# Cross attention: two tiles' output projections in one score slot, a chunk's gate logits in one slot

## What is computed

```python
x = layernorm(x + linear_self_attention(x))          # 2048 rows of 256
x = layernorm(x + cross_attention(x, ctx, ctx))      # 16 heads of 16, 1601 keys
x = layernorm(x + moe(x))                            # 16 experts, the 4 best for a row, and a shared one

def cross_attention(query, key, value):
    Q, K, V = heads(query @ Wq + bq), heads(key @ Wk + bk), heads(value @ Wv + bv)
    attn = softmax(Q @ K.T / 4)
    return merge(attn @ V) @ Wo + bo                 # "@ Wo" is the output projection of the change

probs = softmax(x @ gate_w.T)                        # "x @ gate_w.T" are the gate logits of the change
```

## Time and profile before

| | |
|---|---|
| timed runs, median (lowest to highest of 3) | 1037.9 us (1035.8 to 1038.04) |
| the profiled execution | 1044.55 us, its span 1042.7 us |
| busy: PE, DVE, ACT, POOL | 943.0, 749.9, 646.4, 264.1 us |
| main loop | about 240 to 795 us of the span |
| chunk 1 starts (step 0), chunk 2, chunk 3 | 372.3, 511.7, 653.3 us |
| L1206 PE, a pass of the projection | x48, 0.38 to 0.48 us each |
| L874 ACT, copy of a projection | x12, 0.38 us each |
| L746 POOL, addition of a projection | x8, 0.68 us each (median) |
| L1227 PE, a pass of the logits | x48, 0.26 us each (median) |
| L885 ACT, copy of two tiles' logits | x6, 0.20 us each |

### The profile page before, as it was taken

How to read it: one execution, slowest core, us unless ns; L and a number is a source line. 1 busy time by engine, 2 the same in 40 slices (tenths; PEclk the granted TensorE clock), 3 DMA queues, 4 the chain that set the end, 5 groups by cost and what they waited for, 6 DMA issues and landing times.

```text
span 1042.7 us, 19228 instructions
## 1 busy us (share of the span) xinstructions
PE 943.0 (90%) x6870; PEld 514.8 (49%) x6870; DVE 749.9 (72%) x1230; ACT 646.4 (62%) x1405; POOL 264.1 (25%) x354
## 2 busy tenths in 40 slices
PE   6997899769999999999999999999999999898790
PEld 2453566424444444444444444434434887676660
DVE  0205888598999998989998989988971544333694
ACT  1322233206888888888887888867788565556460
POOL 1006011900000001020012420023243446654564
PEclk9999999957999999999999999999989999999895
DMA  9007895110333434010001110112345354435863
GB/s 347 20 1 136 132 114 138 41 61 1 94 104 100 108 98 125 8 28 22 25 19 49 48 43 18 27 32 75 103 138 153 93 148 138 132 119 150 271 212 136
DMA packets 75508, 99.29 MB, mean 95 GB/s; under 512 B 17276, under 2 KB 58492, under 8 KB 75098
## 3 DMA queue, kind: packets, MB, share of 16 engines
q1 hardware_dynamic: 63960, 73.73, 27.8%
q0 software_dynamic: 7584, 20.79, 5.4%
q10 hardware_dynamic: 3872, 3.56, 1.0%
HBM read 52.45 MB, written 43.35 MB: 92 GB/s over the span
## 4 chain that ended last, share of the span: by engine, by line
PE 65%; DVE 20%; issue 5%; DMA 3%; ACTq 2%; ACT 2%; SPq 1%; POOL 1%; another core or an unknown queue 0%; POOLq 0%; DVEq 0%
PE psum L1182 17%; PE psum L1072 13%; DVE mpart L1485 10%; PE psum L1168 8%; PE psum L1337 7%; PE psum L1355 4%; PE psum L1034 3%; PE psum L1298 2%; PE psum L1001 1%; ACTq L802 1%; PE psum L1122 1%; PE psum L1206 1%; DMA kparts_d<-region 1%; PE psum L1008 1%; PE psum L1196 1%
## 5 line engine op out<-in xcount | busy, mean ns | idle before, releaser
L956 ACT ACTIVATE region<-psum 128x512 f32<-128x512 f32 (+1 forms) x832 | 448.4, 604 | 127.6 <-PE psum L1168 113.0
L1485 DVE TENSOR_REDUCE mpart<-psum 128x2 f32<-128x1024 f32 x384 | 460.1, 1222 | 35.8 <-PE psum L1072 31.8
L1182 PE MATMUL psum<-region 128*32 128x256 f32 (+1 forms) x3120 | 250.5, 393 | 1.8
L1072 PE MATMUL psum<-kstack,qstack 63*128 63x512 f32 (+1 forms) x1024 | 222.4, 462 | 20.7 <-DVE mpart L1485 18.0
L1072 PEld LDWEIGHTS psum<-kstack,qstack 63*128 63x128 f32 x1024 | 92.2, 192 | 194.8 <-issue 125.7
L1168 PE MATMUL psum<-qstack,kstack 64*128 64x512 f32 (+1 forms) x832 | 176.2, 414 | 0.1
L1168 PEld LDWEIGHTS psum<-qstack,kstack 64*128 64x128 f32 (+1 forms) x832 | 111.2, 185 | 17.5 <-ACT region L956 10.7
L1745 DVE SCALAR_TENSOR_TENSOR silu_h<-tanh_h,psum 128x128 f32<-128x128 f32 x110 | 31.6, 287 | 119.8 <-ACT tanh_h L926 89.9
L1182 PEld LDWEIGHTS psum<-region 128*32 128x32 f32 (+1 forms) x3120 | 62.1, 108 | 112.0 <-issue 80.0
L708 POOL DMA_INDIRECT given_d<-y_out,x_in x94 | 93.1, 990 | 84.1 <-ACT y_out L940 59.3
L1337 PE MATMUL psum<-w_all,xT_in 128*128 x376 | 100.0, 389 | 9.5 <-issue 7.1
(11 more groups left out here) (197 smaller groups left out, 955.6 us busy)
## 6 DMA issues: line engine op xcount, KB each, us to landing
x_in<-sorted_d SPq DMA_DIRECT2D x94, 129.0 KB
sorted_d<-x_in SPq DMA_DIRECT2D x7, 1548.0 KB, 7.8
given<-given_d SPq DMA_DIRECT2D x16, 512.0 KB
qstack<-qparts_d SPq DMA_DIRECT2D x96, 64.0 KB, 2.3
kstack<-kparts_d SPq DMA_DIRECT2D x6, 800.5 KB
qparts_d<-region SPq DMA_DIRECT2D x4, 1024.0 KB, 4.1
kparts_d<-region SPq DMA_DIRECT2D x4, 800.5 KB, 10.1
xT<-in_xT SPq DMA_DIRECT2D x1, 2048.0 KB, 8.9
```

What stands on the lines that cost most here:

```text
L956: act.activation(prob[0:rows_of, s % 3, j, :], ring(n)[0:rows_of], ACT.Exp).then_inc(ring_read, 1)
L1072: mm = pe.matmul(bank(unit_bank(u) + side)[:, at * w:(at + 1) * w], qstack[rows_of, buffer(G), p, t * P:(t + 1) * P], kstack[rows_of, g * ...
L1182: mm = pe.matmul(bank(NUM_BANK)[VW * j:VW * (j + 1), q], vals[0:r, g, kt, j, :], prob[0:r, s % 3, j, q], start=(kt == 0 and half == 0), st ...
L1485: dve.tensor_reduce(mpart[:, G % 2, qt, :, p, n], both, X, ALU.max).then_inc(max_read, 1)
```

## The change

Two tiles' projections share a slot. Their results lie side by side in one bank (2 x 256 columns), and ScalarE copies both in one instruction. `PROJ_AT` becomes (12, 18); in chunk 3 the two slots stand at steps 12 and 14. The four tiles' logits share a slot at step 34 (chunks 1 and 2) or 23 (chunk 3), and steps 36 and 24 lose theirs. GpSimd's additions move from steps 13, 16, 19, 22 to 13, 14, 19, 20; VectorE's statistics from 15, 18, 21, 24 to 15, 16, 21, 22. In chunk 3 VectorE's steps stay. The products, the additions and the statistics are the same in number.

```diff
-        PROJ_AT = (12, 15, 18, 21)
+        PROJ_AT = (12, 18)
+        PROJ_TILES = TPC // len(PROJ_AT)
...
-                jobs = ([(12 + t, "proj", t) for t in range(TPC)]
-                        + [(4, "rank", 1), (20, "x2T", 0), (21, "x2T", 1), (23, "logits", 0), (24, "logits", 1),
-                           (32, "rank", 2)])
+                jobs = [(12, "proj", 0), (14, "proj", 1), (4, "rank", 1), (20, "x2T", 0), (21, "x2T", 1),
+                        (23, "logits", 0), (32, "rank", 2)]
             else:
-                jobs = ([(PROJ_AT[t], "proj", t) for t in range(TPC)]
-                        + [(30, "x2T", 0), (32, "x2T", 1), (34, "logits", 0), (36, "logits", 1)]
+                jobs = ([(at, "proj", n) for n, at in enumerate(PROJ_AT)]
+                        + [(30, "x2T", 0), (32, "x2T", 1), (34, "logits", 0)]
...
-                        if at == PROJ_AT[t] + 1:
+                        if at == PROJ_AT[t // PROJ_TILES] + 1 + t % PROJ_TILES:
                             add_attention(c - 1, t)
...
-            def copy_proj(c, t, n):
+            def copy_proj(c, part, n):
+                first, end = PROJ_TILES * part, PROJ_TILES * (part + 1)
                 act.wait_ge(ring_full, n + 1)
                 if c >= 1:
-                    act.wait_ge(co_read, TPC * (c - 1) + t + 1)
-                act.activation(proj[:, t, :], ring(n)[:, 0:DIM], ACT.Copy).then_inc(ring_read, 1)
+                    act.wait_ge(co_read, TPC * (c - 1) + end)
+                act.activation(proj[:, first:end, :].rearrange("p t n -> p (t n)"), ring(n)[:, 0:PROJ_TILES * DIM],
+                               ACT.Copy).then_inc(ring_read, 1)
...
-                for k in range(DK):
-                    mm = pe.matmul(ring(n)[:, 0:DIM], attnT[:, k, t * P:(t + 1) * P], wo_c[:, k, :],
-                                   start=(k == 0), stop=(k == DK - 1))
+                for q in range(PROJ_TILES):
+                    t = PROJ_TILES * part + q
+                    for k in range(DK):
+                        mm = pe.matmul(ring(n)[:, q * DIM:(q + 1) * DIM], attnT[:, k, t * P:(t + 1) * P], wo_c[:, k, :],
+                                       start=(k == 0), stop=(k == DK - 1))
                 mm.then_inc(ring_full, 1)
...
-                for q in range(2):
-                    t = 2 * half + q
+                for t in range(TPC):
                     for k in range(DK):
-                        mm = pe.matmul(ring(n)[:, q * EXPERTS:(q + 1) * EXPERTS], x2T[:, k, t * P:(t + 1) * P],
+                        mm = pe.matmul(ring(n)[:, t * EXPERTS:(t + 1) * EXPERTS], x2T[:, k, t * P:(t + 1) * P],
                                        gate_wT[:, k, :], start=(k == 0), stop=(k == DK - 1))
                 mm.then_inc(ring_full, 1)
...
-                        if at == PROJ_AT[t] + 3:
+                        if at == PROJ_AT[t // PROJ_TILES] + 3 + t % PROJ_TILES:
                             attended_stats(c - 1, t)
```

More of the change, by code:

```diff
@@ L739, in divide @@
                 if c >= 1 and k == 0:
-                    pool.wait_ge(ring_full, extra_slot("proj", (c - 1, TPC - 1)) + 1)
+                    pool.wait_ge(ring_full, extra_slot("proj", (c - 1, len(PROJ_AT) - 1)) + 1)
                 pool.tensor_tensor(attnT[:, k, :], num_c[:, k, :], den_c[:, k, :], ALU.mult).then_inc(attn_ready, 1)
@@ L744, in add_attention @@
                 at = TPC * c + t
-                pool.wait_ge(ring_read, extra_slot("proj", (c, t)) + 1)
+                pool.wait_ge(ring_read, extra_slot("proj", (c, t // PROJ_TILES)) + 1)
                 pool.tensor_tensor(x_sb[:, at, :], proj[:, t, :], x_sb[:, at, :], ALU.add).then_inc(co_read, 1)
@@ L878, in copy_x2T, with copy_logits @@
                 if c >= 1:
-                    act.wait_ge(ring_full, extra_slot("logits", (c - 1, 1)) + 1)
+                    act.wait_ge(ring_full, extra_slot("logits", (c - 1, 0)) + 1)
                 act.activation(x2T[:, k, :], ring(n), ACT.Copy).then_inc(ring_read, 1)
-            def copy_logits(c, half, n):
+            def copy_logits(c, n):
                 act.wait_ge(ring_full, n + 1)
-                at = TPC * c + 2 * half
-                act.activation(logits[:, at:at + 2, :].rearrange("p t e -> p (t e)"),
-                               ring(n)[:, 0:2 * EXPERTS], ACT.Copy).then_inc(ring_read, 1)
+                act.activation(logits[:, TPC * c:TPC * (c + 1), :].rearrange("p t e -> p (t e)"),
+                               ring(n)[:, 0:TPC * EXPERTS], ACT.Copy).then_inc(ring_read, 1)
             def copy_rank(stage, n):
@@ L963, in _ @@
                 elif what == "logits":
-                    copy_logits(*arg, n)
+                    copy_logits(arg[0], n)
                 elif what == "rank":
@@ L1198, in weigh_whole, with out_proj @@
                 mm.then_inc(pv_done, 1)
-            def out_proj(c, t, n):
+            def out_proj(c, part, n):
                 pe.wait_ge(attn_ready, DK * (c + 1))
                 ring_free(n)
-                if c == 0 and t == 0:
+                if c == 0 and part == 0:
                     pe.wait_ge(ld_woc, 16)
-                for k in range(DK):
-                    mm = pe.matmul(ring(n)[:, 0:DIM], attnT[:, k, t * P:(t + 1) * P], wo_c[:, k, :],
-                                   start=(k == 0), stop=(k == DK - 1))
+                for q in range(PROJ_TILES):
[3 more added lines that the diff above has]
+                                       start=(k == 0), stop=(k == DK - 1))
                 mm.then_inc(ring_full, 1)
@@ L1216, in turn_x2, with gate_logits @@
                 mm.then_inc(ring_full, 1)
-            def gate_logits(c, half, n):
+            def gate_logits(c, n):
                 pe.wait_ge(ring_read, extra_slot("x2T", (c, 1)) + 1)
@@ L1365, in behind_scores @@
                 elif what == "logits":
-                    gate_logits(*arg, n)
+                    gate_logits(arg[0], n)
                 elif what == "rank":
@@ L1561, in add_attention @@
                 else:
-                    dve.wait_ge(ring_read, extra_slot("proj", (c, t)) + 1)
+                    dve.wait_ge(ring_read, extra_slot("proj", (c, t // PROJ_TILES)) + 1)
                     change = proj[:, t, :]
@@ L1589, in gate_centre @@
                 else:
-                    dve.wait_ge(ring_read, extra_slot("logits", (c, 1)) + 1)
+                    dve.wait_ge(ring_read, extra_slot("logits", (c, 0)) + 1)
                 link(dve.tensor_reduce(one, logits[:, lo:hi, :], X, ALU.max))
```

## The result

| | before | after |
|---|---|---|
| timed runs, median of 8 (lowest to highest) | 1037.86 us (1035.8 to 1040.66) | 1042.71 us (1038.74 to 1043.85) |
| the profiled execution | 1044.55 us, its span 1042.7 | 1040.94 us, its span 1039.1 |
| main loop, from its first weighing to that of step 38 of chunk 3, in the profiled execution | 522.3 us | 526.3 us |

A forecast was written before the change was run, and what follows sets the result against it. TensorE paces plain steps, VectorE close behind, with 0.65 us of lag forgiven. Terms -1.08 - 0.32 - 0.72 + 1.32 + 0.61 = -0.19 us, taken from the median 1037.9, gave 1037.7 us, range 1035.2 to 1040.5.

The forecast's parts named there:

- a wait of 0.36: Chunks 1 and 2, after step 17: TensorE waits 0.36 us for VectorE behind the statistics of steps 15 and 16.
- The second wait: Chunks 1 and 2, near step 23 or 24: TensorE waits 0.30 us behind the statistics of steps 21 and 22.
- grow by 0.12: Chunks 1 and 2, each: 0.66 us of waits for VectorE, less what the dropped projection slots 15 and 21 save.
- the 0.54 of the slots: Chunks 1 and 2, each: projection slots 15 and 21 go, saving 0.27 us apiece on TensorE.
- grow by 0.29: Chunk 3, steps 12 to 18: VectorE's reads come 0.61 us later, less 0.32 saved by dropping slot 13.
- first rival: TensorE alone counts, lags forgiven: 2.39 us saved, 1035.5 us, 18%; sign: no unit behind steps 16 and 22 waits.
- second rival: No lag tolerance; chunks 1 and 2's statistics cost 4.56 us: 1041.0 us, 12%; sign: steps 16, 17, 22, 23 stretch half a microsecond.
- the third: Rival: a merged tile costs its full slot, +2.2 us, 1040.1 us, 10%; sign: two-tile slots well over 2.0 us.
- something unseen: Whole kernel: the 10% chance left for a cause that neither the forecast nor its three rivals named.
- a slot gone saves 0.24, three times: 0.72 us: Logit slots, one dropped per chunk: eight more passes cost 0.88 us against 1.12 for an own slot.

The follow-up runs named there:

- spaced: The kernel before with projections shared in chunks 1 and 2 only, statistics at their old steps, chunk 3 and logits as before; 1047.87 us, ratio 0.9997.
- after_timed: The changed kernel, unaltered, timed again beside the other runs against the kernel before; 1051.12 us against 1047.18, ratio 1.0024.
- logits_only: The kernel before with the four tiles' logits in one slot a chunk and nothing else of the change; 1049.09 us against 1047.11, ratio 1.0021.
- proj_only: The kernel before with the change's shared projections and moved statistics, logits in two slots as before; 1047.99 us, ratio 1.0019.
- before_again: The kernel before, unaltered, run once more for a second trace; 1051.27 us in one run.

## Why the prediction was wrong

**The terms that it had were right.** Step 12 was to last 4.46 us and does. Step 18 was given about 4.5 us beside a wait of 0.36, and lasts 4.91 (4.92 in two other traces) with a wait of 0.33. The second wait was to be 0.30 and is 0.21. Chunks 1 and 2, steps 12 to 33, were to grow by 0.12 each and grew by 0.12 to 0.21; `spaced` takes the waits away and gets the 0.54 of the slots. Chunk 3, steps 12 to 18, was to grow by 0.29 and grew by 0.25 to 0.30. A logit slot gone saves, where the clock stays, 0.18 and 0.24 us (forecast 0.24). The first rival's sign is absent, since the units do wait; the second's too, since no step stretches by half a microsecond; and two-tile slots cost 1.97, not "well over 2.0", against the third. The second rival's 1041.0 stands nearest to the measured 1042.7, but not by its mechanism; what happened falls under the 10% that were left for something unseen.

**The step that failed** is the term "a slot gone saves 0.24, three times: 0.72 us". It took a slot of sixteen passes for two slots of eight less one gap, and carried the clock of the earlier trace rows over to what follows. Nowhere in the argument is the granted clock of TensorE looked at, though the page of the profile has a row for it. What stands in its place: in the three traces of the changed kernel seven falls' worth of time behind the nine logit slots (2, 2 and 3), at 1.47 us each by the table (11.19 - 9.71 = 1.48, 8.44 - 6.96 = 1.48, 12.67 - 9.71 = 2 x 1.48), which is 3.4 us an execution.

The sum made again from what was measured: +0.64 for projections and statistics, -0.66 for the logit slots, +3.4 for the clock, together +3.4 us. Timed were +4.2 (2.6 to 5.7) and +2.5 (0.2 to 4.8). The logits alone: -0.66 + 3 falls in two traces, 2.2, makes +1.5 against +2.2 timed (0.3 to 4.1).

Seven falls in three traces is a small sample. The timed executions have each a mean granted clock: 0.958 on average over the twelve of `after_timed` and the twelve of `logits_only`, 0.960 over the 20 and the 29 of before beside them, 0.0023 less in both cases, and 0.9597 over the twelve of `proj_only`. By a rough estimate 0.0023 of 1049 us is 2.4 us, so about 2.4 in place of 3.4 for the clock, and the sum is +2.4 us, beside the +2.5 timed. It is rough because this mean takes in every fall of the program: `spaced`, with the logits as before, has 0.959 against 0.961 on its chip.

**What stays open.** Why 6 of 15 narrow slots are spared. Whether the first comparison's +4.2 us owes something to steps 9 to 11 of chunk 3, whose 13.29 us in the first trace of after are a meeting of VectorE and GpSimd and a long fall; its two further traces have 11.91 and 11.90 there, before_again 11.89, and `spaced`, which has the logits as before, 12.69. And the 1.3 us by which the timed middle of proj_only exceeds its steps.

## What to carry to other kernels

Where a change gathers TensorE's narrow products in one place, read the granted clock behind them, in several executions: the gap saved was 0.24 us here, one fall costs 1.5 where TensorE sets the pace. The extra work of an engine that trails the pacing one belongs in small parts, or under a burst that the pacing engine makes anyway; past what the buffers forgive (0.65 us here) it costs its time, and moving it so, with the projections shared in two chunks, made this kernel 6.4 us faster.

## What was not expected of the hardware

The granted clock fell to about 0.5 behind 2 us in which TensorE was 100% busy by the rows: 9 times in 15 with passes of 16 columns, 0 in 6 with 128 columns, 0 in 30 behind 1 us of the narrow ones. The Trainium skill (TensorE: Matmul & The Clock Gate, "HAM oscillation — how this bites in real kernels") ties such falls to stretches in which TensorE idles, waiting for DMA. For steps 9 to 11 of chunk 3 the traces agree in part: before has an idle time of 1.34 us at 679.22 and the fall with it, but VectorE is who is waited for, and `proj_only` has waits of 1.34 and 1.57 us there and no fall. For the logits they don't: there is no idle time in the rows ahead of the fall, and the measurement decides.

A small VectorE operation on 128x16 took 1.20 to 1.28 us in place of 0.17 each time that GpSimd's multiplication of 1.26 us had started up to 0.1 us ahead of it, in 6 traces of 13. VectorE's reads of PSUM that ran beside the same multiplication in before kept their 1.32 us for two. What the two engines hold against each other no run here shows.

Eight passes with eight weight loads took 1.97 us in a slot, and 1.89 from the first pass to the next weighing against 1.03 for four, so the second tile of a projection costs 0.86 us. The rule of the Trainium skill that the prediction weighed (TensorE: Matmul & The Clock Gate, "Part 3: Packing small matmuls", The mechanism), that loads hide only where the row group differs, does not show in these slots.
